# A two-layer decoder on one core: where 32-wide attention turns its output, and the order of work around layer 1's projection

## The reference

```python
# layer 0: 16 heads of width 32, one shared key/value head
Q = (x @ Wq_w.T + Wq_b).reshape(b, l, 16, 32); K = x @ Wk_w.T + Wk_b; V = x @ Wv_w.T + Wv_b
out = softmax(einsum('bqhd,bkd->bhqk', Q, K) / sqrt(32)) @ V
# layer 0's feed-forward: 4-bit weights, silu(gate) * up, down, then y / rms(y)
# layer 1: 16 heads of width 32 with keys and values of their own, qkv from one weight with bias
```

## Time and profile before

| | us |
|---|---|
| median of 3 runs (2604.71 to 2605.39) | 2604.94 |
| profiled execution | 2608.19 |
| its span | 2606.5 |
| PE busy | 2435.3 |
| DVE busy | 1742.4 |
| ACT busy | 1182.4 |
| stretch of layer 0's attention steps | 104 to 380 |
| feed-forward's end | 862 to 889 |
| layer 1's projections | 889 to 1050 |
| stretch of layer 1's attention steps | 1050 to 1330 |

### The profile page before, as it was taken

One profiled execution on the slowest core, in us unless ns is written; L12 is line 12 of the kernel. 1 busy time (PEld: TensorE's weight loads), 2 busy tenths in 40 slices (PEclk: granted clock), 3 DMA queues, 4 the chain that ended last, 5 costly groups with the idle time before them and its releaser, 6 DMA issues. The chain is left out here.

```text
span 2606.5 us, 38233 instructions
## 1 busy us (share of the span) xinstructions
PE 2435.3 (93%) x11324; PEld 1763.3 (68%) x11324; DVE 1742.4 (67%) x3696; ACT 1182.4 (45%) x2318; POOL 156.9 (6%) x263
## 2 busy tenths in 40 slices
PE   7999998799999899999996999999999999999679
PEld 6555556677777677555564777777777777777457
DVE  6577777778887744666656566676676666666643
ACT  3466765333333522666632445444444444444221
POOL 0000000100000000000030010101010100000100
PEclk9899999899999999999999999999999999999789
DMA  5622200000000225443201000000000000000101
GB/s 170 185 73 64 73 1 1 1 1 0 0 0 1 91 92 179 117 94 88 60 1 48 18 12 8 12 12 16 4 16 4 16 4 16 12 0 0 42 1 65
DMA packets 71227, 104.10 MB, mean 40 GB/s; under 512 B 14091, under 2 KB 27147, under 8 KB 71019
## 3 DMA queue, kind: packets, MB, share of 16 engines
q1 hardware_dynamic: 71146, 103.08, 13.5%
HBM read 73.16 MB, written 29.88 MB: 40 GB/s over the span
## 5 line engine op out<-in xcount | busy, mean ns | idle before, releaser
L3147 DVE SCALAR_TENSOR_TENSOR x_res<-xa_out_bank,xa_den,x_res 128x512 f32 (+1 forms) x256 | 191.3, 747 | 157.3 <-PE xa_out_bank L2787 157.1
L499 DVE TENSOR_REDUCE l1s_mx<-l1s_max_bank 128x1 f32<-128x512 f32 x256 | 159.7, 675 | 85.4 <-PE l1s_max_bank L355 85.3
L3056 ACT ACTIVATE xa_pT_hi<-xa_t_bank 128x512 fp32r<-128x512 f32 x256 | 149.5, 597 | 126.0 <-PE xa_t_bank L2924 126.0
L499 DVE TENSOR_REDUCE l0s_mx<-l0s_max_bank 128x1 f32<-128x512 f32 x256 | 160.0, 675 | 60.2 <-PE l0s_max_bank L355 60.1
L3067 ACT ACTIVATE xa_prob<-xa_prob,xa_nmax 128x512 f32<-128x512 f32 x256 | 182.6, 715 | 30.1 <-DVE xa_nmax L3129 30.1
L2787 PE MATMUL xa_out_bank<-xa_o_w,xa_o_hi 128*128 128x512 f32 x512 | 175.3, 424 | 22.4 <-DVE x_res L3147 20.9
L3111 DVE TENSOR_TENSOR xa_pT_lo<-xa_t_bank,xa_pT_hi 128x512 fp32r<-128x512 f32 x256 | 175.5, 686 | 23.2 <-ACT xa_pT_hi L3056 19.1
L3129 DVE CUSTOM_DVE_ANT_0 xa_prob<-xa_s_bank,xa_mask_bias 128x512 f32<-128x512 f32 x256 | 171.1, 686 | 20.2 <-PE xa_s_bank L2787 9.7
L2173 DVE SCALAR_TENSOR_TENSOR ffn_yT<-ffn_y,ffn_ysc,ffn_yT 128x512 f32<-128x512 f32 x176 | 129.3, 745 | 46.8 <-PE ffn_y L1921 46.7
L2924 PE MATMUL xa_t_bank<-ident,xa_prob 128*128 128x128 f32 x1024 | 150.6, 275 | 0.0
L2924 PEld LDWEIGHTS xa_t_bank<-ident,xa_prob 128*128 128x128 f32 x1024 | 121.0, 141 | 39.7 <-issue 18.0
(11 more groups left out here) (477 smaller groups left out, 5856.6 us busy)
## 6 DMA issues: line engine op xcount, KB each, us to landing
l0s_q<-l_q SPq DMA_DIRECT2D x96, 128.0 KB, 2.4
l1s_q<-l_q SPq DMA_DIRECT2D x96, 128.0 KB, 3.2
l1s_k<-l_k SPq DMA_DIRECT2D x96, 128.0 KB, 3.5
l0s_k<-l_k SPq DMA_DIRECT2D x96, 64.0 KB, 2.5
x_res<-in_x_dram SPq DMA_DIRECT2D x4, 1024.0 KB, 9.7
l_q<-l_q_hi SPq DMA_DIRECT2D x16, 256.0 KB, 2.6
l_q<-l_q_lo SPq DMA_DIRECT2D x16, 256.0 KB, 3.2
l_q<-l_hi SPq DMA_DIRECT2D x16, 256.0 KB, 2.1
```

The costliest lines, as they stand in the source:

```text
L499: dve.tensor_reduce(self.mx[:, j // QT, j % QT:j % QT + 1], self.max_bank[(2 * s + j) % 3][:], AX.X, ALU.max)\
L3056: act.activation(pT_hi[:, kt % (QT - 1), :], t_bank[kt % 2][:], ACT.Copy).then_inc(pT_hi_done, 1)
L3147: dve.scalar_tensor_tensor(xt, out_bank[:], den[:, r, 2, q:q + 1], xt, ALU.mult, ALU.add)\
```

## The change

Attention, for both layers: the rows of the maxima go to max_bank 2 instead of t_bank, so the banks of the maxima are counted by j % 3 in every step, and the rows wait for the sixth reduction of the step. The turn of the output of p - 1 moves from the end of step p to behind its fifth score. VectorE takes invert, normalise and add_out of p - 1 behind its eight reductions (it was p - 2, amid them). The preparing rings in the last two steps have two banks. In both layers the rows of pair 0 are turned after all maxima of pairs 0 and 1.

Feed-forward's end: two of the four first adds into x move behind the last h_lo; the last adds into y stand among the statistics; ScalarE's last four squares come after the x tiles and the first two weights; VectorE takes the low parts of these two weights before the last mean squares. These four squares write their unused product elsewhere.

Layer 1's projection: after projection 0 of batch 0 two weights are turned, then one each, with two after projections 4 and 5; the kept adds into x are one per projection; the statistics and the x tiles of the next batch come later or earlier as the diff says.

```diff
@@ PairAttention.maximum, max_rows, turn, tensor, rows, reduce
-        reached(pe, self.max_read, 8 * p + j - 2)
-        pe.matmul(self.max_bank[(2 * s + j) % 3][:], self.qs[s][0:self.STK, n, q * P:(q + 1) * P],
+        if j < 3:
+            reached(pe, self.mrow_ready, 2 * (p - 1) if j == 2 else 0)
+            reached(pe, self.max_read, 8 * p - (1, 0, 2)[j])
+        else:
+            pe.wait_ge(self.max_read, 8 * p + j - 2)
+        pe.matmul(self.max_bank[j % 3][:], self.qs[s][0:self.STK, n, q * P:(q + 1) * P],
...
-        reached(pe, self.o_read, p - 2)
+        pe.wait_ge(self.max_read, 8 * (self.NP if self.late(p, 2) else p + 2) - 2)
         for q in range(QT):
-            last = pe.matmul(self.t_bank[0:HD + 2, q * P:(q + 1) * P],
+            last = pe.matmul(self.max_bank[2][0:HD + 2, q * P:(q + 1) * P],
...
         pe.wait_ge(self.oT_ready, p + 1)
-        pe.wait_ge(self.mrow_ready, 2 * self.NP if self.late(p, 2) else 2 * (p + 3))
-        if self.late(p, 2):
-            pe.wait_ge(self.o_read, p)
+        reached(pe, self.o_read, p)
...
                 self.score(pe, p, s, k)
+                if k == 4 and not self.early(p, 1):
+                    self.turn(pe, p - 1)
...
-            if not self.early(p, 1):
-                self.turn(pe, p - 1)
@@ PairAttention.vector
-            reducing, done = not self.late(p, 2), not self.early(p, 2)
-            for j in range(8):
-                if reducing:
+            reducing, done = not self.late(p, 2), not self.early(p, 1)
+            if reducing:
+                for j in range(8):
                     self.reduce(dve, p + 2, (s + 2) % self.R, j)
-                if done and j == 3:
-                    self.invert(dve, p - 2)
-                if done and j == 4:
-                    self.normalise(dve, p - 2)
+            elif beside:
+                beside(p - self.NP + 2)
+            if done:
+                self.invert(dve, p - 1)
             if reducing:
                 self.split_max(dve, p + 2, s)
-            elif beside:
-                beside(p - self.NP + 2)
-            if not self.early(p, 2):
-                self.add_out(dve, p - 2)
+            if done:
+                self.normalise(dve, p - 1)
+                self.add_out(dve, p - 1)
@@ layer 0, ahead of the steps
-        fa_ring = Ring(st, "fac", att.max_bank, fa_jobs)
+        fa_ring = Ring(st, "fac", att.max_bank[0:2], fa_jobs)
...
-                att.max_rows(pe, 0, 0)
                 maxima(1, range(1, 4))
                 project(B - 1, 4)
                 maxima(1, range(4, 8))
+                att.max_rows(pe, 0, 0)
...
-                for f in range(NF - 1):
+                for f in range(NF):
                     take(B - 1, f)
                 att.rows(act, 0, 0)
-                take(B - 1, NF - 1)
@@ Layer1
-        for f in range(2, KC):
-            self.after[0][f - 2] = [("w", f)]
-        for f in range(KC, self.QK):
-            self.after[0][f - 2] = [("w", f)]
-        for n in range(2):
-            self.after[0][self.QK - 2 + n] = [("w", self.QK + 2 * n), ("w", self.QK + 2 * n + 1)]
+        for n, weights in enumerate(((2, 3), (4,), (5,), (6,), (7, 8), (9, 10), (11,))):
+            self.after[0][n] = [("w", f) for f in weights]
         for b in range(B - 1):
             for q in range(QT):
-                self.after[b][(self.QK if b == 0 else KC) + q].append(("x", b + 1, q))
+                self.after[b][self.QK - (0 if b == 0 else 2) + min(q, 2)].append(("x", b + 1, q))
...
-                    if n == self.NT - 2:
-                        att.max_rows(pe, 0, 0)
+        att.max_rows(pe, 0, 0)
...
-                    if n == 1 or n == 2:
+                    start = 2 if b == 0 else 0
+                    if start <= n < start + 2:
...
@@ four_bit_ffn, ScalarE
                 for q in range(QT):
                     front.ring.take_hi(act, front.at["x", 0, q])
-                    if q % 2:
-                        late_square(3 * QT + q - 1)
-                        late_square(3 * QT + q)
+                for f in range(2):
+                    front.ring.take_hi(act, front.at["w", f])
+                for t in range(3 * QT, T):
+                    late_square(t)
                 root(2)
@@ four_bit_ffn, VectorE
                             inverses(0)
-                            for t in range(2):
-                                add_x(t)
+                            add_x(0)
...
                         if last_step:
-                            for t in range(2, QT):
-                                add_x(t)
+                            add_x(1)
...
+                for t in range(2, QT):
+                    add_x(t)
+                last = (NC - 1) % 2
                 for t in range(QT):
                     wait_added(t)
                     front.norm.tile_stats(dve, t)
-                last = (NC - 1) % 2
-                add_y(NC - 1, last, B - 1, 0)
-                add_y(NC - 1, last, B - 1, 1)
+                    if t:
+                        add_y(NC - 1, last, B - 1, t - 1)
                 front.norm.combine(dve, 0, batch_tiles(0))
-                add_y(NC - 1, last, B - 1, 2)
                 add_y(NC - 1, last, B - 1, 3)
...
                 add_x(KEPT + 1)
+                for f in range(2):
+                    front.ring.take_lo(dve, front.at["w", f])
                 mean_squares(2)
-                front.ring.take_lo(dve, front.at["w", 0])
                 inverses(2)
...
                 def add_kept(n):
-                    if n < 3:
-                        for t in range(QT + 2 * n, QT + 2 * n + 2):
-                            add_x(t)
+                    if n < 4:
+                        add_x(QT + n)
+                    elif n in (7, 8):
+                        add_x(QT + n - 3)
```

More of the change, by code:

```diff
@@ L467, in rows @@
         for n in range(2):
-            act.activation(self.qs[s][self.STK:self.STK + 2, n, :], self.t_bank[HD * n:HD * n + 2, :], ACT.Copy)\
+            act.activation(self.qs[s][self.STK:self.STK + 2, n, :], self.max_bank[2][HD * n:HD * n + 2, :], ACT.Copy)\
                 .then_inc(self.mrow_ready, 1)
@@ L498, in reduce @@
         dve.wait_ge(self.maxed, 8 * p + j + 1)
-        dve.tensor_reduce(self.mx[:, j // QT, j % QT:j % QT + 1], self.max_bank[(2 * s + j) % 3][:], AX.X, ALU.max)\
+        dve.tensor_reduce(self.mx[:, j // QT, j % QT:j % QT + 1], self.max_bank[j % 3][:], AX.X, ALU.max)\
             .then_inc(self.max_read, 1)
@@ L554, in vector @@
         self.rounds(dve, step)
-        for p in range(self.NP - 2, self.NP):
-            self.invert(dve, p)
-            self.normalise(dve, p)
-            self.add_out(dve, p)
+        self.invert(dve, self.NP - 1)
+        self.normalise(dve, self.NP - 1)
+        self.add_out(dve, self.NP - 1)
 def persistent(st):
@@ L1604, in __init__ @@
         self.ring = Ring(st, "l1r", self.att.max_bank[0:2], jobs)
-        self.out_ring = Ring(st, "l1o", self.att.max_bank,
+        self.out_ring = Ring(st, "l1o", self.att.max_bank[0:2],
                              [([self.ow_raw[:, f, c * P:(c + 1) * P] for f in range(KC)],
@@ L1725, in scalar @@
         att = self.att
-        self.ring.take_hi(act, self.at["w", 0])
-        self.ring.take_hi(act, self.at["w", 1])
         act.wait_ge(self.bias_loaded, 16)
@@ L1736, in scalar @@
                                    bias=self.bias[:, n:n + 1]).then_inc(self.hi_done, 1)
-                if n == 3 and b + 1 < B:
+                if n == (4 if b == 0 else 3) and b + 1 < B:
                     self.norm.root(act, b + 1, batch_tiles(b + 1))
@@ L1775, in vector @@
                 if b + 1 < B:
-                    if n == 1 or n == 2:
+                    start = 2 if b == 0 else 0
+                    if start <= n < start + 2:
                         for q in range(2):
-                            wait_added(QT * (b + 1) + 2 * (n - 1) + q)
-                            self.norm.tile_stats(dve, QT * (b + 1) + 2 * (n - 1) + q)
-                    if n == 2:
+                            wait_added(QT * (b + 1) + 2 * (n - start) + q)
+                            self.norm.tile_stats(dve, QT * (b + 1) + 2 * (n - start) + q)
+                    if n == start + 2:
                         self.norm.combine(dve, b + 1, batch_tiles(b + 1))
-                    if n == 4:
+                    if n == start + 4:
                         self.norm.scales(dve, b + 1)
                         self.normalise(dve, b + 1, range(2))
-                    if n == 5:
+                    if n == start + 5:
                         self.normalise(dve, b + 1, range(2, QT))
@@ L1860, in four_bit_ffn @@
         KEPT = T - len(late)
+        unused = [w[:].rearrange("p (k c) -> p k c", k=KC) for w in h32 + sl]
         ADDED = tuple(range(QT)) + tuple(range(KEPT, T)) + tuple(range(QT, KEPT))
@@ L2070, in square @@
                 def square(t, source):
```

(17 more changed lines are left out.)

## The result

The changed kernel takes 2575.84 us (median of 4 runs, 2573.15 to 2578.1) beside 2605.16 for the kernel before, run with it: a ratio of 0.9884 (times after over before), 95% interval 0.9870 to 0.9898, 29.3 us faster. The profiled execution took 2575.5, span 2573.8.

A forecast was written before the change was run, and what follows sets the result against it. TensorE, busy 93% of the span, was taken as the bound, with attention steps a loop over TensorE and VectorE. Terms -18.8 - 1.3 + 4.0 + 0.1 + 0.65 - 6.2 + 1.2 gave -20.3: 2584.6 us, range 2576 to 2597.

The forecast's parts named there:

- Layer 1's projection: Layer 1's projection: weights turned further ahead remove most TensorE waits and some low-clock loss, -6.2 us (bounds -8.0 and -2).
- Steps: Both attentions' steps: the turn hides behind reductions, a step becomes 8.31 us (bounds 8.21 and 8.50), -18.8 us in all.
- Start of layer 0: Start of layer 0's attention: TensorE stands 2.0 us and the first score comes later, +4.0 us (bounds +3.3 and +7).
- Feed-forward's end: Feed-forward's end to layer 1's first projection: two adds delay it 1.4, late squares return 0.75, +0.65 us.
- SP's later loads: Layer 1's projection: SP loads the attention's pieces 2.75 us later, delaying q's store, +1.2 us (bounds 0 and 2.75).
- Ends of the attentions: Last two steps and ends of both attentions: earlier turns gain, layer 0's two-bank ring loses, -1.3 us in sum.
- (a): Rival on attention steps: rows behind a wait need 0.57 us to the weighing, steps 8.50, 2598 us; chance 0.12.
- (b): Rival on layer 1's projection: VectorE is late at each weight, -2 instead of -6.2, 2589 us; chance 0.13.
- (d): Rival on attention steps: they stay as they are since the reductions alone set them, 2603 us; chance 0.04.
- (c): Rival on attention steps: TensorE's pauses drop its clock to the low level, slower than before, 2621 us; chance 0.03.

The follow-up runs named there:

- e3: The kernel before with only x of the next batch turned later in batches 1 and 2: 2600.57 us, ratio 0.9973.
- e2: The kernel before with only the feed-forward's end and layer 1's projection as changed, attention as before: 2596.76 us, ratio 0.9959.
- e4: The changed kernel with the output's turn back at the end of a step: 2600.57 us, ratio 0.9980 to the kernel before.
- e10: The changed kernel with the rows of the maxima, from pair 1 on, in a score bank, waiting for the sixth exponential: 2575.0 us, ratio 0.9877.
- e11: e9 with two waits on the finished maxima moved to the output's turn and product in the written-out steps: 2563.77 us, ratio 0.9837.
- e1: The kernel before with only the attention part changed, including both starts and the two-bank rings: 2584.26 us, ratio 0.9915.
- e7: The changed kernel with the rows of the maxima behind the first pair of weighing matmuls: 2589.12 us, ratio 0.9935 to the kernel before.
- e8: The changed kernel with e9's two edits and e7's edit together: 2586.99 us, ratio 0.9925 to the kernel before.
- e9: The changed kernel with first adds into x ahead of the last hidden product and pair 0's rows right behind projection 3: 2568.51 us, ratio 0.9859.

## Why the prediction was right in direction and missed the range

**The step that failed is "Layer 1's projection".** It took its waits from the earlier trace rows, batch 0 and the start of batch 1. The edit that moves x's turns in batches 1 and 2 was put at nothing, but for its consequence for SP. The two stands of 2.85 us in front of x's first tile were in the trace, one in each batch, and no term holds them. That is -5.3 of the 8.8 us between forecast and median, shown by e3 and again by e2. With them the forecast would have been 2579.3. The term for batch 0 was near (-6.2, measured -7.3): there no wait over 1 us is left, where two of 0.9 had been expected.

**Steps: right in the turn, size 3.2 short.** The turn is hidden (e4: +0.4 per step without that). The chain weighing, first maximum, six reductions, rows, weighing ends where it was placed, but in the loop TensorE's own stream ends at the same time, and the step stays 8.22 where the rows don't wait for the sixth reduction (e10). The prediction took the brackets of the weight loads for TensorE's waits: the 0.37 of the earlier trace rows is 0.1 in the starts of the matmuls, one of several such delays that add to 0.46 per step. 8.31 came from the earlier trace rows, which is a written-out step: its first reduction starts 0.61 behind the maximum's load. In the loop it is 0.54, the rows follow the sixth reduction 0.06 sooner (0.06 behind its end for 0.12), and steps are 8.22, at the lower bound of 8.21. The written-out steps are 8.35. e11 shows what the difference is: two waits on one instruction. So 36 of the steps gained 0.41, 20 gained 0.35 (one of them more). That one is the step with statistics on VectorE, which was to lose 0.35 and gained 0.71: 8.35 like its neighbours, for 9.06.

**Start of layer 0: +4.0 expected.** The first score came at 99.90 (expected 100.0) and the stand at 86.6 came, 2.19 long; but 1.9 of this first score's delay lie ahead of the attention, where nothing was edited. Over all traces the cost is 2.3. No low clock was added in the profiled execution of the changed kernel (0.70 in the stretch from 94 to 104), but it was in three of the six traces with this start, right behind the stand, as had been feared.

**Feed-forward's end: +0.65 expected, +2.8 measured** (e2: +2.8). The two adds cost 1.1 to 1.4 and the other orders gave back 0.3 to 0.6, where 0.75 had been expected. What the sum had no term for is the 2.0 of the y turns at TensorE's low level, in four of six kernels with this order.

**SP's later loads: +1.2 expected, 0.4 at most came.** Batch 3 is 0.4 longer with the orders alone (e2, e3) and 0.5 shorter in the changed kernel, where the attention's part takes 0.7 off (e1). SP started the 24 loads 7.8 us ahead of batch 3 instead of 8.5, not 2.75 later, since before they had waited for the stores of k; and SP's own pause among them was shorter. ScalarE's third copy of q waits as in the earlier trace rows, 10.8 us into batch 3 for 11.0 (timeline of the changed kernel):

```profile
1004.82 0.69 ACT L1727 ACTIVATE l_hi<-l1s_score_bank,l_bias 128x512 fp32r<-128x512 f32 x1 [4.27 <-DMA l_q<-l_lo]
```

**Ends of the attentions: -1.3 expected, -1.0 measured.** Layer 0's last two steps lost 1.3 (expected 0.9), layer 1's won 0.9, each end 0.7. In layer 0 the last turn now waits for the end's copy alone (timeline of the changed kernel, for the earlier trace rows); the idle time of 1.58 holds the last weighing's matmuls too.

```profile
370.79 0.42 PEld L400 LDWEIGHTS l0s_t_bank<-ident,l0s_oT 128*128 128x128 f32 x4 [1.58 <-ACT l0s_oT L476]
```

**The rivals.** (a), a full stream of 0.57 behind a wait: no, 0.36, so 8.22 and not 8.50. (b), little from the projection: no. (d), steps unchanged: no. (c), the clock swinging in the steps, did not come: the granted clock of 230 us of steps is 1.00 in the changed kernel, e1, e4, e7, e8, e9, e10 and e11. This is no strong test, since TensorE hardly stands in a loop step of the changed kernel; the steps of the kernel before, with 0.46 of delays each, are at 1.00 as well. The Trainium skill, "TensorE: Matmul & The Clock Gate", section "A second HAM failure mode: psum-queue depth-cycling", says that small idle times between groups of matmuls that cycle through PSUM banks can make the clock swing; no trace here shows it for delays as small as these.

## What to carry to other kernels

When an edit moves the same operation in several rounds of a loop, look for the wait in front of it in each round; here a list of TensorE's waits over the whole stretch had the two that were left out of the sum. Size a loop's step from a loop's step: a written-out one carries other waits. And before a wait is removed, read the starts of the matmuls beside those of the weight loads: here the 0.24 us for VectorE lay in time in which TensorE still streamed the last score, so taking it away gave nothing (e10), and moving the rows cost 0.26 per step (e7).

## What the runs showed of the hardware that wasn't expected

- In these kernels a wait for a second semaphore that was reached long ago isn't free: the late one then stands as an instruction of its own and costs about 0.07 us where it is on the chain. Two of them made a step 8.35 instead of 8.22, and moving them to instructions with slack gave 8.22 (e11).
- Idle time in the row of weight loads isn't idle time of TensorE. Behind each step's weighing the loads stand 0.81 us and at the step's end 0.24, and over both the matmuls go on: by their starts in the changed kernel it is 0.53 from the last pair of weighing matmuls to the first maximum, where such pairs stand 0.43 apart, and 0.23 from the last score to the rows.
- Four small matmuls (128x34 weights) cost 0.24 us between a score and the weighing and 0.52 among the weighing's own matmuls (changed kernel and e7).
- The same code around the feed-forward's end took 18.6 or 16.6 us, at nearly the same mean granted clock (0.82, and 0.79 to 0.82). The difference is which work the low level covered: the turns of four y tiles took 3.3 us at 0.50 and 1.7 at 1.00.
